# Queries and keys stored in an order in which one row of operands is one run of memory

## What is computed

```python
def _lora(x, W, A, Bm):
    return x @ W.T + x @ Bm.T @ A.T * LORA_SCALING
q = _lora(x, Wq, Aq, Bq).reshape(B, T, H, dh).transpose(0, 2, 1, 3)
k = _lora(x, Wk, Ak, Bk).reshape(B, T, H, dh).transpose(0, 2, 1, 3)
s = jnp.einsum('bhqd,bhkd->bhqk', q, k) / jnp.sqrt(jnp.float32(dh))
s = s + bias[None]
s = jnp.where(j[None, None] <= i[None, None], s, NEG_INF)
out = jnp.einsum('bhqk,bhkd->bhqd', jax.nn.softmax(s, axis=-1), v)
x = _layernorm(x + _L0_attn_ref(x, L0_attn_Wq, ...), axis=-1)
x = _layernorm(x + _L0_ffn_ref(x, L0_ffn_Wg, ...), axis=-1)
```

## Time and profile before

| | |
|---|---|
| median of 3 runs (lowest to highest) | 1346.04 us (1344.16 to 1349.74) |
| the profiled execution | 1345.55 us |
| its span, first to last instruction | 1343.8 us |
| start-up, until the first scores | 0 to 40.6 us |
| TensorE busy | 1164.5 us (87%) |
| ScalarE busy | 918.9 us (68%) |
| VectorE busy | 676.8 us (50%) |

### The profile page before, as it was taken

The page is one execution under the profiler, slowest core; times in us unless marked ns, Lnnn a source line. Parts: engine busy times, 40 slices in busy tenths (PEclk is TensorE's granted clock), DMA queues, the critical chain, the costliest instruction groups (busy, mean ns, idle before and its releaser), DMA issues. The chain is left out here.

```text
span 1343.8 us, 24544 instructions
## 1 busy us (share of the span) xinstructions
PE 1164.5 (87%) x8759; PEld 503.3 (37%) x8759; DVE 676.8 (50%) x1791; ACT 918.9 (68%) x1195; POOL 353.4 (26%) x382
## 2 busy tenths in 40 slices
PE   7788989999988999799999989526999999999990
PEld 3222222222222222122222211014877877787780
DVE  4434323232556545645455400264677576677756
ACT  2488889999887999698989989314354344444314
POOL 2321121111112223040403310032525534543430
PEclk9799999999999999999999999857999999999995
DMA  6833232423321222030402100245135333422216
GB/s 153 152 86 85 72 71 75 93 60 84 80 58 58 85 63 75 17 105 17 117 5 82 32 10 6 84 140 169 22 105 122 65 78 105 100 37 26 26 22 250
DMA packets 81733, 103.80 MB, mean 77 GB/s; under 512 B 12922, under 2 KB 66917, under 8 KB 81617
## 3 DMA queue, kind: packets, MB, share of 16 engines
q1 hardware_dynamic: 64496, 77.28, 21.1%
q0 software_dynamic: 15744, 23.83, 8.4%
q10 hardware_dynamic: 1376, 1.18, 0.6%
HBM read 56.76 MB, written 48.06 MB: 78 GB/s over the span
## 5 line engine op out<-in xcount | busy, mean ns | idle before, releaser
L1330 ACT ACTIVATE prob<-ps_s 128x1024 f32<-128x1024 f32 (+3 forms) x854 | 721.3, 980 | 101.9 <-PE ps_s L1234 100.5
L1250 PE MATMUL ps_o<-prob,v_aug 128*17 128x512 f32 (+3 forms) x3294 | 422.6, 575 | 29.0 <-DVE acc L1390 18.3
L1234 PE MATMUL ps_s<-qop,kop 51*128 51x512 f16 (+3 forms) x1647 | 267.1, 372 | 26.8 <-ACT prob L1330 8.9
L1390 DVE COPY acc<-ps_o 32x512 f32<-32x512 f32 (+1 forms) x116 | 79.7, 687 | 307.7 <-PE ps_o L1250 300.1
L1234 PEld LDWEIGHTS ps_s<-qop,kop 51*128 51x128 f16 x1647 | 62.4, 94 | 404.9 <-ACT prob L1330 360.1
L2047 PE MATMUL ps_y<-w2s,hs 128*128 128x256 bf16 (+1 forms) x1728 | 199.5, 273 | 1.2 <-DVE yb L2124 1.2
L1356 POOL TENSOR_SCALAR_AFFINE_SELECT prob<-prob 128x256 f32<-128x256 f32 (+1 forms) x180 | 69.4, 394 | 476.8 <-ACT prob L1330 472.6
L2094 ACT ACTIVATE hid<-ps_h,b 128x384 f32<-128x384 f32 (+1 forms) x192 | 105.0, 559 | 120.0 <-PE ps_h L2031 95.0
L2031 PE MATMUL ps_h<-xs,w1s 128*128 128x384 bf16 (+1 forms) x1152 | 182.4, 318 | 5.0 <-ACT hid L2094 4.2
L2047 PEld LDWEIGHTS ps_y<-w2s,hs 128*128 128x128 bf16 (+1 forms) x1728 | 167.4, 99 | 19.0 <-DVE yb L2124 1.5
L1988 POOL DMA_INDIRECT result<-y,entry x72 | 112.0, 1556 | 179.4 <-DVE y L2129 148.4
(11 more groups left out here) (159 smaller groups left out, 696.3 us busy)
## 6 DMA issues: line engine op xcount, KB each, us to landing
w<-in_W SPq DMA_DIRECT2D x16, 1024.0 KB, 7.6
slots_x<-empty POOLq DMA_DIRECT2D x12, 520.0 KB, 3.9
qop<-fparts_q SPq DMA_DIRECT2D x42, 128.0 KB, 5.0
xe<-slots_x SPq DMA_DIRECT2D x8, 650.0 KB
x_all<-in_xT SPq DMA_DIRECT2D x8, 512.0 KB, 5.0
attnT<-acc SPq DMA_DIRECT2D x128, 32.0 KB
aT<-attnT SPq DMA_DIRECT2D x16, 256.0 KB
x_all<-in_x SPq DMA_DIRECT2D x8, 512.0 KB
```

The costliest lines, as they stand in the source:

```text
L1234: mm = pe.matmul(ps_s[:, u.p % SLOTS_S, e, a.q0:], o.key(e, a.h, a.kt), o.query(e, a.h, a.b, a.q0), start=True, stop=True)
L1250: mm = pe.matmul(ps_o[c:c + VW, a.q0:], o.v[:, a.kt, a.h], prob[:, t % RING, n, e, a.q0:], start=a.first, stop=a.last)
L1330: act.activation(prob[:, t % RING, n, e:z, q0:], ps_s[:, u.p % SLOTS_S, e:z, q0:], ACT.Exp, scale=1.0 / (SCALE * SCALE)).then_inc(exp_done, 1)
L1390: dve.tensor_copy(acc[rows, a], ps_o[rows]).then_inc(evicted[job.lane], 1)
```

## The change

The scratch tensors get the shape (8 blocks, 2 parts, 32 rows, 8 pairs, 512 tokens): a row is one channel of one half, and its 8 pairs of a block stand next to each other, 8 KB in one run. The projection makes channels in the order half, channel, pair, by permuting the columns of `weff` while VectorE sums them; the swap of heads 6 and 7 is done there too. A tile is stored in two transfers, one for each part. A load of a block takes two transfers for each half in place of three: for the keys one of 32 rows (both parts, whose source has two outer steps, one for each part) and one of 16; for the queries one of 16 and one of 32. `hsel` is made by VectorE from the identity matrix in place of its load, and SP's load of `xT` for block 2 moves behind the stores of block 1. The path that is not taken (`General`) is adapted to the new order of channels.

```diff
+TP = P // (2 * DH)
+STANDS = [[[next(h for h in (2 * i, 2 * i + 1) if ROW_HALF[h] == e) for i in range(TP * c, TP * (c + 1))] for e in range(2)]
+          for c in range(2)]
...
     def load_keys(o, eng, fparts, b):
-        for s, (_, pk) in enumerate(FPARTS):
-            src = fparts["k"][pk].rearrange("(i e d) t -> e d i t", e=2, d=DH)
-            for e in range(2):
-                eng.dma_start(o.k[b][HALF * e + 16 * s:HALF * e + 16 * s + 16],
-                              src[e][:, FIRST_PAIR[b]:, b * QB:(b + 1) * QB]).then_inc(o.k_loaded[b % 2], 16)
+        for e in range(2):
+            row = HALF * e
+            for s, (pk, z) in ((0, (0, 2)), (2, (0, 1))):
+                for_rows = o.k[b][row + 16 * s:row + 16 * (s + z - pk)]
+                eng.dma_start(for_rows, fparts["k"][b, pk:z, 16 * e:16 * e + 16, FIRST_PAIR[b]:]).then_inc(o.k_loaded[b % 2], 16)
...
     def load_queries(o, eng, fparts, b):
-        for s, (pq, _) in enumerate(FPARTS):
-            src = fparts["q"][pq].rearrange("(i e d) t -> e d i t", e=2, d=DH)
-            for e in range(2):
-                eng.dma_start(o.q[HALF * e + 16 * s:HALF * e + 16 * s + 16, b % 2],
-                              src[e][:, :, b * QB:(b + 1) * QB]).then_inc(o.q_loaded[b % 2], 16)
+        for e in range(2):
+            row = HALF * e
+            for s, (pq, z) in ((0, (0, 1)), (1, (0, 2))):
+                eng.dma_start(o.q[row + 16 * s:row + 16 * (s + z - pq), b % 2],
+                              fparts["q"][b, pq:z, 16 * e:16 * e + 16]).then_inc(o.q_loaded[b % 2], 16)
...
-        j.fparts = {m: dram(f"fparts_{m}", (2, D, T), F16) for m in "qk"}
+        j.fparts = {m: dram(f"fparts_{m}", (NB, 2, 2 * DH, NP_, QB), F16) for m in "qk"}
...
-        dst = j.fparts["qk"[m // 2]][:, (m % 2) * P:(m % 2 + 1) * P, n * QB:(n + 1) * QB].rearrange("a p t -> p a t")
-        for a, z, to in j.ROWS[m % 2]:
-            sp.dma_start(dst[to:to + z - a], j.part[a:z, m]).then_inc(j.stored[m], 16)
+        for a in range(2):
+            sp.dma_start(j.fparts["qk"[m // 2]][n, a, :, TP * (m % 2):TP * (m % 2 + 1)], j.part[:, m, a]).then_inc(j.stored[m], 16)
...
+                if m < 2:
+                    lora, w = (x.rearrange("p (i e d) -> p i e d", e=2, d=DH) for x in (lora, w))
+                    out = out.rearrange("p (g e d i) -> p g i e d", g=2, e=2, i=TP)
+                    for to, at in ((out[:, 0, 0:3], (slice(0, 3),)), (out[:, 0, 3, 1], (3, 0)), (out[:, 0, 3, 0], (3, 1))):
+                        dve.scalar_tensor_tensor(out=to, in0=lora[(slice(None), *at)], scalar=LORA_SCALE * scale,
+                                                 in1=w[(slice(None), *at)], op0=ALU.mult, op1=ALU.add).then_inc(j.weff_done, 1)
+                    out, lora, w = out[:, 1], lora[:, TP:], w[:, TP:]
...
+    def dve_hsel(j, dve):
+        dve.wait_ge(j.small_loaded, 16)
+        dve.wait_ge(j.hsel_set, 1)
+        dve.tensor_reduce(j.hsel[:, 0:2 * TP].rearrange("p (e i) -> p e i", e=2), j.ident[:].rearrange("p (e d i) -> p e i d", e=2, i=TP),
+                          AX.X, ALU.max).then_inc(j.hsel_set, 1)
...
                 j.load_keys(sp, 0)
-                j.load_x(sp, 2)
                 for k in range(4):
                     j.store(sp, 1, k)
+                j.load_x(sp, 2)
```

More of the change, by code:

```diff
@@ L96 @@
 ROW_HALF = [1 - h % 2 if h in SWAPPED else h % 2 for h in range(H)]
+STANDS = [[[next(h for h in (2 * i, 2 * i + 1) if ROW_HALF[h] == e) for i in range(TP * c, TP * (c + 1))] for e in range(2)]
+          for c in range(2)]
+ORDER = [STANDS[c][e][i] * DH + d for c in range(2) for e in range(2) for d in range(DH) for i in range(TP)]
 Tile = namedtuple("Tile", "b h kt q0 diag first last")
@@ L394, in query @@
         return o.q[HALF * e:HALF * e + FROWS, b % 2, h // 2, q0:]
-    K_LOADS = 16 * (2 * len(FPARTS) + 2)
-    Q_LOADS = 16 * 2 * len(FPARTS)
+    K_LOADS = 16 * (2 * 2 + 2)
+    Q_LOADS = 16 * 2 * 2
     def load_keys(o, eng, fparts, b):
-        for s, (_, pk) in enumerate(FPARTS):
-            src = fparts["k"][pk].rearrange("(i e d) t -> e d i t", e=2, d=DH)
-            for e in range(2):
-                eng.dma_start(o.k[b][HALF * e + 16 * s:HALF * e + 16 * s + 16],
-                              src[e][:, FIRST_PAIR[b]:, b * QB:(b + 1) * QB]).then_inc(o.k_loaded[b % 2], 16)
+        for e in range(2):
[3 more added lines that the diff above has]
+                eng.dma_start(for_rows, fparts["k"][b, pk:z, 16 * e:16 * e + 16, FIRST_PAIR[b]:]).then_inc(o.k_loaded[b % 2], 16)
     def load_bias(o, eng, bias, b):
@@ L411, in load_queries @@
     def load_queries(o, eng, fparts, b):
-        for s, (pq, _) in enumerate(FPARTS):
-            src = fparts["q"][pq].rearrange("(i e d) t -> e d i t", e=2, d=DH)
-            for e in range(2):
-                eng.dma_start(o.q[HALF * e + 16 * s:HALF * e + 16 * s + 16, b % 2],
-                              src[e][:, :, b * QB:(b + 1) * QB]).then_inc(o.q_loaded[b % 2], 16)
+        for e in range(2):
[3 more added lines that the diff above has]
+                              fparts["q"][b, pq:z, 16 * e:16 * e + 16]).then_inc(o.q_loaded[b % 2], 16)
 class Project:
-    ROWS = [[(0, 6 * DH, 0), (6 * DH, 7 * DH, 7 * DH), (7 * DH, P, 6 * DH)], [(0, P, 0)]]
     def done(j, n, k, h=1):
@@ L430, in stores @@
     def stores(j, m, n):
-        return 16 * len(j.ROWS[m % 2]) * n
+        return 16 * 2 * n
     def __init__(j, io, sb, sem, dram, flag, o, r, spare, first):
         j.io, j.flag, j.o, j.r = io, flag, o, r
-        j.fparts = {m: dram(f"fparts_{m}", (2, D, T), F16) for m in "qk"}
+        j.fparts = {m: dram(f"fparts_{m}", (NB, 2, 2 * DH, NP_, QB), F16) for m in "qk"}
         j.bias = dram("bias", (NB, H, 3, QB), F16)
@@ L504, in load_weights @@
             j.load_x(sp, n)
-        sp.wait_ge(j.hsel_set, 1)
-        sp.dma_start(j.hsel[:, 0:8], io["headsel"]).then_inc(j.small_loaded, 16)
         sp.dma_start(j.ident[:], io["ident"]).then_inc(j.small_loaded, 16)
@@ L648, in dve_weights @@
             for c in range(2):
-                dve.scalar_tensor_tensor(out=j.weff[:, m, c, 0:D], in0=banks(3 + m)[:, c * D:(c + 1) * D],
-                                         scalar=LORA_SCALE * scale, in1=j.wT[:, m, c, :], op0=ALU.mult,
-                                         op1=ALU.add).then_inc(j.weff_done, 1)
+                lora, w, out = banks(3 + m)[:, c * D:(c + 1) * D], j.wT[:, m, c, :], j.weff[:, m, c, 0:D]
+                if m < 2:
[5 more added lines that the diff above has]
+                    out, lora, w = out[:, 1], lora[:, TP:], w[:, TP:]
+                dve.scalar_tensor_tensor(out=out, in0=lora, scalar=LORA_SCALE * scale, in1=w, op0=ALU.mult,
+                                         op1=ALU.add).then_inc(j.weff_done, 1)
+    def dve_hsel(j, dve):
[3 more added lines that the diff above has]
+                          AX.X, ALU.max).then_inc(j.hsel_set, 1)
     def dve_less(j, dve, k, bank):
@@ L660, in dve_split_weights @@
         if k == 0:
-            dve.wait_ge(j.weff_done, 6)
+            dve.wait_ge(j.weff_done, 18)
             dve.tensor_copy(j.ws[:, 0], w).then_inc(j.ws_high, 1)
@@ L759 @@
     UNITS = 2 * KT
+    STORES = 16 * 2 * TP
     def __init__(y, nc, io, sem, dram, attnT, sums, j, o, prob, ps_s, ps_o, r):
@@ L872, in sync @@
                     sp.wait_ge(y.parted, 3 * (tb * 4 + m + 1))
-                    dst = y.parts["qk"[m // 2]][:, (m % 2) * P:(m % 2 + 1) * P, tb * QB:(tb + 1) * QB]
-                    sp.dma_start(dst.rearrange("a p t -> p a t"), y.part[:]).then_inc(y.stored, 16)
-            sp.wait_ge(y.stored, 16 * 4 * NB)
+                    dst = y.parts["qk"[m // 2]][:, :, tb * QB:(tb + 1) * QB].rearrange("a (h d) t -> h d a t", d=DH)
+                    for e in range(2):
+                        for i in range(TP):
+                            first = HALF * e + i
+                            sp.dma_start(dst[STANDS[m % 2][e][i]], y.part[first:HALF * (e + 1):TP]).then_inc(y.stored, 16)
+            sp.wait_ge(y.stored, y.STORES * 4 * NB)
             with sp.Fori(0, NG) as g:
@@ L996, in vector @@
                 if n >= 1:
-                    dve.wait_ge(y.stored, 16 * n)
+                    dve.wait_ge(y.stored, y.STORES * n)
                 dve.tensor_scalar(y.part[:, 0], y.ps_p, scale, None, ALU.mult).then_inc(y.parted, 1)
@@ L1207, in _ @@
                 j.pe_lora(pe, banks)
-                pe.wait_ge(j.weff_done, 2)
+                pe.wait_ge(j.weff_done, 8)
                 pe.wait_ge(j.w_loaded, 16 * 4)
@@ L1212, in _ @@
                         if n == 0 and k == 2:
-                            pe.wait_ge(j.weff_done, 4)
+                            pe.wait_ge(j.weff_done, 16)
                         if n == 1:
@@ L1217, in _ @@
                     if n == 0:
-                        pe.wait_ge(j.weff_done, 6)
+                        pe.wait_ge(j.weff_done, 18)
                         for s in range(KT):
@@ L1222, in _ @@
```

(3 more changed lines are left out.)

## The result

The changed kernel takes 1366.87 us (median of 4 runs, 1364.84 to 1371.09) against 1345.10 for the kernel before on the same chip: ratio 1.0163, 95% interval 1.0124 to 1.0203. It is slower by 21.8 us, clear of noise; whether by more than 2% the interval leaves open. The forecast was 1355, with 1341 to 1363 as its range: the direction and the main mechanism were right, the size under half of what came. The profiled execution is the longest of the four, 1371.09 us with a span of 1369.3, 25.5 more than before.

The account below looks back on a forecast made before the run. TensorE, busy 87%, bounds it; its 5.7 us wait for block 0's queries was the place. Start 25.7 + 21.5 + 1.5 + 1.0 = 49.7 for 40.59, so 1345.55 + 9.1 = 1354.7: forecast 1355 us, range 1341 to 1363.

Parts of the forecast that it names:

- What bounds the kernel: End of start-up: the first scores waited 5.7 us for block 0's queries; their shift moves the end about as much.
- The two-part loads go to two engines: Loads of 32 rows with a source count of two use 2 of 16 DMA engines; chance 0.70.
- When they begin: Block 0's key loads issued at 23.68 + 0.9 (weight sums) + 0.3 (stores) = 24.9, data moving from 25.7.
- Engine time 21.5 and crossing 1.5: Block 0 on two engines: 20.2 us for two-part loads, 1.3 for one-part; block 1's stores crossing them add 1.5.
- Landing: End of block 0's loads: 1.0 us to land, giving first scores at 49.7 in place of 40.59.
- Later blocks: Loads after block 0 land in time: 5 us to spare in block 1, 13.0 of 15.9 in block 2; cost 0.
- sixteen engines: Rival: the 32 rows set the engine count, two-part loads move 252 GB/s, first scores at 35.8; 1338.6, chance 0.15.
- long runs alone are no quicker: Rival: all 16 engines work but loads stay at 126 GB/s; -1.4 us, 1344.2, chance 0.08.
- The third: Rival: two engines fall below 21 GB/s each, so later blocks wait for their loads too; 1373, chance 0.07.

Follow-up runs that it names:

- rows32b: The changed kernel with scratch memory laid out half before part, so a two-part load counts 32 rows in one stride; 16 stores a block: 1346.28 us, ratio 1.0024.
- two_first: The changed kernel with the two-part loads issued ahead of the one-part loads in each key and query load: 1369.07 us, ratio 1.0168.
- q_last: The changed kernel with block 7's query load issued behind the router's loads of block 6: 1362.17 us, ratio 1.0126.
- s_all: The changed kernel with every two-part load split into two loads of one part and 16 rows, in all blocks: 1349.50 us, ratio 1.0030.
- rows32c: The changed kernel with memory in groups of four pairs: loads of 32 rows in one stride, 4 KB runs, 8 stores a block: 1341.74 us, ratio 0.9981.
- s_start: The changed kernel with two-part loads split into loads of 16 rows in blocks 0 and 1 alone: 1351.83 us, ratio 1.0050.

## Why the prediction was wrong

By its own steps:

- *What bounds the kernel.* Right: the one wait for queries was the place.
- *The two-part loads go to two engines.* Right: a share of 0.13 with them alone, and 0.96 when only the outermost count was changed (`rows32b`). The Trainium skill's rule (*DMA: Bandwidth & Descriptors*, "Why a DMA increments its semaphore by 16 and not by 1": the largest number up to 16 that divides both slowest counts) gave two, and the trace agrees with its 2.1.
- *When they begin.* 25.19 for the issue against 24.9. The weight sums cost PE 0.73 against 0.9 (VectorE took 2.9 us for them after 2.07, +0.8 where I had 1.2 to 1.6); the eight stores took 5.1 us to issue, 0.63 each. Data moved at 26.7, not 25.7: 1.0 short.
- *Engine time 21.5 and crossing 1.5.* Mis-sized by 2.7: 25.7 us, from 26.7 to 52.4, where the last long packet ends. The rate of 25.9 GB/s an engine was right (27 at 46:52). Wrong was to let the two engines have it from the beginning and charge the one-part loads 1.3 us: until 31, for 4.3 us, both kinds together moved at the 16-row rate, in whichever order they were issued (`two_first`). The load of `xT`, said to be out of the way, came at 41.53, into the middle.
- *Landing.* 0.8 against 1.0. Together 53.15 against 49.7: +12.56 in place of +9.1, inside the bounds of +7.0 to +15.8.
- *Later blocks: "Cost 0, as long as an engine keeps its rate."* This is the step that failed. The engines kept their rate (27 GB/s each at 46:52) and no later scores waited for a load of keys or queries, and it cost 5.8 to 8.5 us all the same. I asked when each of these loads would land and when it is needed, and not what else stands behind it: a transfer spread over 16 engines has two parts on the two full ones, and SP issues late behind them, so the router's load of `x` for block 6 was late by both (`q_last`), by the parts most. The margin of block 1 was overrated too: its first scores start at 81.73 without a wait, but the sum had its loads in by 74, and the last count of its queries' semaphore comes at 81.61, 0.1 us ahead of the scores in place of 5. Block 2's queries took 14.2 us from issue to landing where I had 13.0.
- *The end of the kernel.* I did not think that 13 instructions more on VectorE could cost anything 1,100 us later. They bring 2.8 us of waits in place of 0.7; from block 7's first scores to the end it is 1.8 us more.

12.6 + 8.5 + 1.8 = 22.9 of the 25.5 us between the two profiled executions. Another 2.5 lie between the first scores of blocks 3 and 4 (turns 78 and 126), where the changed kernel's granted clock was 0.70 at 206.5:214.5 and that of before 1.00 from 193.9 on; in `q_last` and `two_first`, with the same loads, that stretch takes 88.5 us in place of 90.8, so it isn't the loads' doing. Elsewhere it is 0.1. The median of the changed kernel is 4.2 below its profiled execution, so some of this, the clock above all, is not in every run. By medians, splitting the loads of the start is worth 15.0 us, that of the later ones 5.5, and both together 17.4 (`s_all`).

The rivals: sixteen engines would give 1338.6, and do, once the outermost count is 32: first scores at 36.2 against 35.8, and 1341.7 us (`rows32c`; 1340.1 to 1340.7 with memsets). In `rows32b` the dearer stores took most of that back. That long runs alone are no quicker is what `s_all` shows. The third, two engines and waits of later blocks, named the right kind of loss with the wrong mechanism; its condition, less than 21 GB/s an engine, was not seen where the rate can be read (27).

## What to carry to other kernels

Before making runs longer, count the outermost step of both sides of a transfer: merge it into one stride of 16 or more; without that, the two-part loads here ran on two engines. For a load that takes longer, ask what stands behind it in the issuing queue and on its engines, not only who waits for its data; put short urgent loads ahead. And add a do-nothing control when a change shifts instructions: a few us at a far place may belong to the place of the program.

## What was not expected of the hardware

- A queue's issue stalls behind full engines: four stores took 8.03 us to issue and two loads 8.40, against 2.54 and 0.61 otherwise, while the DMA share was 0.13 to 0.18 at 36:42 and 46:52.
- A transfer over 16 engines is as late as its busiest engine: two of 16 parts landed some 12 us behind the other 14 (`s_start`, 649:650).
- A store whose two sides have different shapes cost SP 0.63 us to issue, against 0.43 in the same queue before (1.74 for four); that the shapes are the reason is not tested alone.
- The rate of these loads follows the rows written, not the run: 16 rows 126 to 137 GB/s with 8 KB runs; 32 rows 207 to 229 with 4 KB, 205 with 8 KB (`rows32b`).
- Instruction loads can be waited for. In the changed kernel VectorE stood still 3.07 and 1.40 us near 1144 (the profile puts the first down to a DMA and the second to nothing that it shows), with four packets of instruction loads in the window, and PE waited 2.8 us behind it. The Trainium skill (*Runtime: NRT & Kernel Launch*, "Instruction fetch mechanics") calls the cost of crossing into the next block mostly hidden and says that a taken branch breaks the prefetch. At this one place the fetch was not hidden, and whether a branch is the reason no run shows.
